# q and k stacked in device memory with one load per head, channel-mix pieces ended in their own step, and two banks each for up and down pieces in the tail

## The reference, cut to what matters

```
x2 = x + time_out                       # time mix
xc = ln(ln(x2)); xcs = shift(xc)
kc = square(relu(xcs @ Wck))            # 512 -> 2048, "up"
vc = kc @ Wcv                           # 2048 -> 512, "down"
A  = x2 + sigmoid(xc @ Wcr) * vc
q, k, v = rms(xn) @ Wq.T, Wk.T, Wv.T    # 16 heads of 32
attn = softmax(causal(q @ k.T / sqrt(32)))
x  = xn + (attn @ v) @ Wo.T             # "proj"
B  = x + sum over 2 of 8 experts of p_e * Wd_e(silu(Wg_e r) * (Wu_e r)),  r = rms(x)
```

## Time and profile before

| | |
|---|---|
| median of 3 runs | 2160.09 us (2159.92 to 2160.28) |
| the profiled execution's own time | 2173.18 us |
| its span | 2171.3 us |
| PE busy | 1872.4 us (86%) |
| PE weight loads busy | 1594.3 us (73%) |
| DVE, ACT, POOL busy | 1172.8, 1055.6, 524.8 us |
| mean granted clock of TensorE | 0.95 |
| phases, by the trace | time mix to about 270 us, projections to 435.7, heads to 1344.6, experts to the end |

### The profile page before, as it was taken

The page is one execution under the profiler, slowest core; times in us unless marked ns, Lnnn a source line. Parts: engine busy times, 40 slices in busy tenths (PEclk is TensorE's granted clock), DMA queues, the critical chain, the costliest instruction groups (busy, mean ns, idle before and its releaser), DMA issues. The chain is left out here.

```text
span 2171.3 us, 30573 instructions
## 1 busy us (share of the span) xinstructions
PE 1872.4 (86%) x10866; PEld 1594.3 (73%) x10866; DVE 1172.8 (54%) x1866; ACT 1055.6 (49%) x1758; POOL 524.8 (24%) x560
## 2 busy tenths in 40 slices
PE   3878679938989888989988754999999999999997
PEld 2666468726767766777766533999999999999986
DVE  6887332135667556666565423555555555555553
ACT  4454344223656555565655312555555555555553
POOL 3243200000000100100100151334344443534343
PEclk9989879969999999999999987999999999999999
DMA  4332345486354433743443314666666665756562
GB/s 174 117 116 97 137 173 193 153 275 142 101 144 114 113 105 112 159 123 100 107 112 101 90 25 148 221 203 204 197 208 209 206 214 196 229 202 205 192 193 49
DMA packets 124211, 334.38 MB, mean 154 GB/s; under 512 B 33743, under 2 KB 33743, under 8 KB 109858
## 3 DMA queue, kind: packets, MB, share of 16 engines
q1 hardware_dynamic: 101266, 291.69, 39.1%
q0 software_dynamic: 18272, 33.13, 9.3%
q10 hardware_dynamic: 4592, 8.52, 1.1%
HBM read 270.67 MB, written 75.06 MB: 159 GB/s over the span
## 5 line engine op out<-in xcount | busy, mean ns | idle before, releaser
L48 PE MATMUL bank<-ex_x_hi,ex_w_hi 128*128 128x256 f32 x1472 | 418.9, 285 | 5.2 <-issue 5.2
L50 PE MATMUL bank<-ex_x_hi,ex_w_lo 128*128 128x256 f32 x1472 | 417.2, 283 | 0.0
L49 PE MATMUL bank<-ex_x_lo,ex_w_hi 128*128 128x256 f32 x1472 | 417.2, 283 | 0.0
L1865 DVE TENSOR_TENSOR ex_w_lo<-ex_stage,ex_w_hi 128x2048 fp32r<-128x2048 f32 x138 | 249.9, 1838 | 147.6 <-ACT ex_w_hi L1810 144.6
L48 PEld LDWEIGHTS bank<-ex_x_hi,ex_w_hi 128*128 128x128 f32 x1472 | 282.9, 192 | 8.2 <-issue 5.6
L49 PEld LDWEIGHTS bank<-ex_x_lo,ex_w_hi 128*128 128x128 f32 x1472 | 283.1, 192 | 2.7
L50 PEld LDWEIGHTS bank<-ex_x_hi,ex_w_lo 128*128 128x128 f32 x1472 | 282.9, 192 | 0.0
L1750 POOL TENSOR_TENSOR ex_a_lo<-ex_a,ex_a_hi 128x256 fp32r<-128x256 f32 x184 | 177.6, 986 | 391.6 <-ACT ex_a_hi L1830 391.1
L1825 ACT ACTIVATE ex_gate<-bank 128x256 f32<-128x256 f32 x184 | 70.7, 384 | 240.0 <-PE bank L50 240.0
L1214 ACT ACTIVATE hd_p_full<-bank 128x512 f32<-128x512 f32 (+1 forms) x192 | 94.4, 528 | 140.7 <-PE bank L1506 139.9
L48 PE MATMUL bank<-hd_down_hi,hd_a_hi 128*128 128x512 f32 x256 | 112.1, 438 | 47.7 <-issue 22.8
(11 more groups left out here) (265 smaller groups left out, 4434.4 us busy)
## 6 DMA issues: line engine op xcount, KB each, us to landing
ex_stage<-in_w_moe SPq DMA_DIRECT2D x69, 1536.0 KB, 6.8
first_w<-in_w_moe SPq DMA_DIRECT2D x23, 1536.0 KB, 7.3
hd_raw<-in_w_up SPq DMA_DIRECT2D x64, 256.0 KB, 2.9
hd_raw<-in_w_dn SPq DMA_DIRECT2D x64, 256.0 KB, 2.8
hd_q<-scratch_q_hi SPq DMA_DIRECT2D x128, 64.0 KB, 2.6
hd_k<-scratch_k_hi SPq DMA_DIRECT2D x128, 64.0 KB, 2.5
tm_x_in<-in_x SPq DMA_DIRECT2D x4, 1024.0 KB, 7.5
scratch_xn<-tm_xn SPq DMA_DIRECT2D x4, 1024.0 KB, 5.2
```

Of the source, the lines that this page charges most:

```text
L48: pe.matmul(out, lhsT=w_hi, rhs=x_hi, start=first, stop=False)
L49: pe.matmul(out, lhsT=w_hi, rhs=x_lo, start=False, stop=False)
L50: return pe.matmul(out, lhsT=w_lo, rhs=x_hi, start=False, stop=last)
L1865: return dve.tensor_tensor(dst, src, hi.bitcast(F32), ALU.subtract)
```

## The change

Scratch tensors q_hi, q_lo, k_hi, k_lo become one, qk, laid out by sequence, part of a bank's rows, stacked row (96), column of heads, q or k, and token. project_phase stores into it with 24 transfers of 256 KB from 32 partitions per sequence where there were 4 of 1 MB: q_hi and k_hi are written twice. load_slot reads a head with one transfer of 384 KB (96 partitions, 4 KB each). SP's list at the start of heads_phase is put in another order, and the waits for constants move to their first use. ACT and DVE finish each piece right after its begin, in its own step, and ACT takes the relu before the weights. The tail's ups alternate between banks 5 and 4, its sums between banks 6 and 0, and PE waits for the piece before last there. The first down (and proj) of four waits for weights and blocks one by one.

```diff
+    TAIL = proj_at[B - 1]
     def turn_bank(b, j):
-        return psum[7] if b < B - 1 else psum[j]
+        return psum[7] if b < B - 1 else psum[1 + j % 3]
-        q2 = sb("q2", [P, SLOTS, S], F32R)
-        k2 = sb("k2", [P, SLOTS, S], F32R)
+        qk = sb("qk", [P, SLOTS, 2, S], F32R)
+        q2, k2 = qk[:, :, 0, :], qk[:, :, 1, :]
+        def up_bank(k):
+            return psum[4] if k >= TAIL and ups_before[k] % 2 else psum[5]
+        def sum_bank(k):
+            return psum[0] if k >= TAIL and sums_before[k] % 2 else psum[6]
# sync, heads_phase
             def load_slot(g):
-                (six transfers of 64 KB)
+                b, c, part = feature_rows(g)
+                sp.dma_start(qk[0:STACK, g % SLOTS, :, :].bitcast(F32), d["qk"][b, part, :, c]).then_inc(slot_in[g % SLOTS], 16)
+            load_slice(0)
             load_slot(0)
-            for w in range(RAW):
-                load_slice(w)
+            load_slice(1)
+            load_mix(0)
+            load_slice(2)
+            load_slice(3)
             load_slot(1)
-            load_mix(0)
-            for g in range(2, SLOTS):
-                load_slot(g)
+            load_slice(4)
+            load_slice(5)
+            for w in range(DEEP):
+                sp.wait_ge(w_lo_ready, w + 1)
+                load_slice(w + RAW)
+                load_slot(w + 2)
             (vecs, wr)
+            for g in range(DEEP + 2, SLOTS):
+                load_slot(g)
             (v, xn, gate)
-            for w in range(DEEP):
-                sp.wait_ge(w_lo_ready, w + 1)
-                load_slice(w + RAW)
# scalar: begin(k) takes the relu before the weights; the loop over steps
-                for k in late:
-                    finish(k)
                 for k in ks[:1]:
                     begin(k)
+                    finish(k)
                 (exps(i, 0), exps(i, 1))
-                for k in ks[:1]:
-                    finish(k)
                 ...
                 for k in ks[1:]:
                     begin(k)
+                    finish(k)
                 (max_row)
-                late = ks[1:]
# vector: the same; finish(k) of the first piece now ahead of maxima(s, 2) and low_v
# tensor
-                n = ups_before[k]
+                n = ups_before[k] - (k > TAIL + TT)
+                if k >= TAIL and n == ups_before[TAIL]:
+                    pe.wait_ge(o_ready, N // 2)
                 if n:
                     pe.wait_ge(a_full, n)
-            def total(k, left_hi, left_lo, j):
-                n = sums_before[k]
+            def total(k, left_hi, left_lo, j, ready):
+                n = sums_before[k] - (k > TAIL)
                 ...
                 for q in range(DEEP):
+                    if j == 0:
+                        ready(q)
             def down(k, b, c, j):
-                pe.wait_ge(w_lo_ready, slice_at["down", b, c, DEEP - 1] + 1)
-                pe.wait_ge(a_lo_ready, ups_before[k])
+                def ready(q):
+                    pe.wait_ge(w_lo_ready, slice_at["down", b, c, q] + 1)
+                    pe.wait_ge(a_lo_ready, ups_before[k] - DEEP + q + 1)
-            pe.wait_ge(consts_ready, CONSTS)
-            pe.wait_ge(const_in, 32)
# sync, project_phase
-            def features_out(name, src, b, out):
-                sp.dma_start(d[name][b].rearrange("c p s -> p c s"), src[:, :, :].bitcast(F32)).then_inc(out, 16)
+            def features_out(src, which, groups, b, out):
+                for part in range(HC):
+                    for g in groups:
+                        sp.dma_start(d["qk"][b, part, g * HD:(g + 1) * HD, :, which, :],
+                                     src[part * HD:(part + 1) * HD, :, :].bitcast(F32)).then_inc(out, 16)
```

More of the change, by code:

```diff
@@ L772, in feature_rows @@
         half, c, place = n // 8, n % 8 // 2, n % 2
-        return b, c, (half * 2 + place) * HD
+        return b, c, half * 2 + place
     def pair_cols(p):
@@ L997, in load_slot @@
             def load_slot(g):
-                b, c, row = feature_rows(g)
-                src = slice(row, row + HD)
-                for n, (qs, ks) in enumerate((("q_hi", "k_hi"), ("q_hi", "k_lo"), ("q_lo", "k_hi"))):
-                    at = slice(n * HD, (n + 1) * HD)
-                    sp.dma_start(q2[at, g % SLOTS, :].bitcast(F32), d[qs][b, c, src, :]).then_inc(slot_in[g % SLOTS], 16)
-                    sp.dma_start(k2[at, g % SLOTS, :].bitcast(F32), d[ks][b, c, src, :]).then_inc(slot_in[g % SLOTS], 16)
+                b, c, part = feature_rows(g)
+                sp.dma_start(qk[0:STACK, g % SLOTS, :, :].bitcast(F32), d["qk"][b, part, :, c]).then_inc(slot_in[g % SLOTS], 16)
             def load_v(p):
@@ L1068, in _ @@
                     load_xn(b)
-            for k in range(pieces_before(STEPS), PIECES):
+            for k in range(TAIL, PIECES):
                 follow(k)
@@ L1161, in begin @@
             def begin(k):
-                for w in fresh[k]:
-                    weight(w)
                 kind, b, c, m = order[k]
@@ L1167, in begin @@
                     act.wait_ge(up_done, n + 1)
-                    act.activation(relu[:, m, :], up_bank[:, :], ACT.Relu).then_inc(relu_ready, 1)
+                    act.activation(relu[:, m, :], up_bank(k)[:, :], ACT.Relu).then_inc(relu_ready, 1)
+                for w in fresh[k]:
+                    weight(w)
                 if k in turn_at:
@@ L1258, in _ @@
                 weight(w)
-            act.wait_ge(consts_ready, CONSTS)
-            act.wait_ge(const_in, 32)
-            late = []
             for s in range(STEPS):
@@ L1442, in _ @@
                 weight(w)
-            dve.wait_ge(consts_ready, CONSTS)
-            late = []
             for s in range(STEPS):
@@ L2049, in _ @@
                 sp.wait_ge(q_hi_ready, b * HC + HC)
-                features_out("q_hi", q_hi, b, q_hi_out)
+                features_out(q_hi, 0, (0, 1), b, q_hi_out)
                 sp.wait_ge(q_lo_ready, b * HC + HC)
-                features_out("q_lo", q_lo, b, q_lo_out)
+                features_out(q_lo, 0, (2,), b, q_lo_out)
                 sp.wait_ge(k_hi_ready, b * HC + HC)
-                features_out("k_hi", k_hi, b, k_hi_out)
+                features_out(k_hi, 1, (0, 2), b, k_hi_out)
                 sp.wait_ge(k_lo_ready, b * HC + HC)
-                features_out("k_lo", k_lo, b, k_lo_out)
+                features_out(k_lo, 1, (1,), b, k_lo_out)
                 sp.wait_ge(v_ready, b * TT + TT)
                 sp.dma_start(d["v"][b], v[:, :, :]).then_inc(v_out, 16)
-            for out in (q_hi_out, q_lo_out, k_hi_out, k_lo_out, v_out):
-                sp.wait_ge(out, 16 * B)
+            for out, copies in ((q_hi_out, 8), (q_lo_out, 4), (k_hi_out, 8), (k_lo_out, 4), (v_out, 1)):
+                sp.wait_ge(out, 16 * copies * B)
         @block.gpsimd
@@ L2096, in high @@
                     if b and m == 0:
-                        act.wait_ge(out, b * 16)
+                        act.wait_ge(out, b * 16 * 8)
                     act.activation(dst[:, m, :], psum[bank + m][:, :], ACT.Copy).then_inc(ready, 1)
@@ L2147, in low @@
                     if b and m == 0:
-                        dve.wait_ge(out, b * 16)
+                        dve.wait_ge(out, b * 16 * 4)
                     dve.tensor_tensor(dst[:, m, :], psum[bank + m][:, :], hi[:, m, :].bitcast(F32),
```

45 lines of the change are left out of this document (28 added, 17 removed).

## The result

| | before | changed |
|---|---|---|
| median, same chip (4 runs each) | 2160.01 us (2158.37 to 2160.28) | 2103.49 us (2099.81 to 2107.55) |
| the profiled execution's own time, its span | 2173.18, 2171.3 us | 2101.72, 2099.6 us |
| PE, DVE, ACT, POOL busy | 1872.4, 1172.8, 1055.6, 524.8 us | 1864.0, 1176.2, 1055.2, 520.0 us |
| mean granted clock | 0.95 | 0.956 |

What follows compares the result with a forecast made beforehand. Heads phase limits: late constants at the start, PE in the steps, a PE-ACT-DVE-PE bank chain in the tail, then POOL. From the median, 2160.1 - 20 + 2 - 32 - 2 - 26.5 = 2081.6, said as 2082 us; range 2058 to 2114.

Steps and rivals of the forecast that it cites:

- the wait for exps' third part: Heads steps, ACT: a wait for the third part of the turned scores would appear, under 0.5 us.
- The start: Start of heads phase: first up at about 446 instead of 466.25 us, released by the mix input; 20 us gained.
- The stores: Last projections sequence: more, narrower q and k stores delay v's store and the phase end by 0 to 6, taken as 2 us.
- Pieces end in their own step: Heads steps: earlier a_lo and block waits 28, clock 12, relu 4, less ACT's new wait 12; 32 us gained (5 to 44).
- the 12 of the clock: Heads steps, 520 to 1150 us: 12 of 19 us lost to lower granted clock go with PE's waits.
- The new wait of ACT: Heads steps: ACT waits after relu for DVE's a before exps(i, 0); 12 us lost over 59 steps (0 to 35).
- The tail: End of heads phase: second banks and earlier scatter make it 111 us against 151.7; 26.5 us gained without the 14.1.
- The 14.1 us: Tail: PE's 15.65 us wait less its usual 1.50, taken as belonging to the profiled execution alone and left out.
- the rival of the long wait: Tail: the long wait is in ordinary runs too and goes with the second bank; 2068 us, chance 0.12.
- ACT eating the middle: Heads steps: ACT's new wait costs 0.5 us or more per step, middle gains only about 10 us; 2104 us, chance 0.16.
- The stores' rival: Projections: port limits make stores cost 5 us in the last sequence and each of three others; 2100 us, chance 0.08.
- lock: Heads steps: ACT, DVE and PE wait in one ring, 1.5 us more per step, 88 us lost; 2170 us, chance 0.04.

Runs made afterwards that it cites:

- start alone: Kernel before with only SP's new start order and the constants' waits moved to first use, on chip A: 2174.26 us, ratio 0.9962.
- coarse waits: Changed kernel, but a chunk's first down waits at its start for the whole chunk, not block by block, on chip C: 2148.98 us, ratio 0.9836.
- the late one: Changed kernel with a step's second piece finished at the next step's start: 2119.00 us (A); with whole-chunk waits too, 2161.71 us (C).

## Why the prediction was right or wrong

The time fell inside the range, 21.5 us above the forecast: 56.5 us were gained where 78 were forecast. The direction and the four places of the gain were right. That the time stayed inside owes something to luck and to the range's width, for all three signs that the prediction named for being wrong came: PE's idle time in the steps is 58.2 us (43.2 of the 610 from 510 to 1120), not under 40; the scatter starts 50.8 us into the tail, later than 48; and v's store lands 8.0 us late, more than 6. Kept were the signs of the releaser, the downs (no wait for a_lo over 0.8 us), the clock (0.99) and the scatter without a gap; the wait for exps' third part reached 0.9 us, not under 0.5.

- **The start.** 18.7 us to the first up, forecast 20. Right as a step, and the releaser is the mix input as forecast; x_lo took 9.7 us to land, just outside the 7.3 to 9.3 of the earlier trace rows. (It is issued fifteen issues earlier in SP's list, not seven; the time of 2 us behind the phase's first issue was right.) What the sum left out: 6.8 us of an earlier start alone are given back within the stage (start alone). "So nothing is late" was wrong: slices are, ACT waits 16 to 18 us for one. That the copies of x make them late is not shown by the total: with the copies moved that stall goes, and the stage is 0.7 us shorter.
- **The stores.** Forecast 2 us in a range of 0 to 6, measured 8.1 between the first two traces, of which 7.1 behind the projections' first product, and 6.1 over all: the memset at 446.9 as the mean of nine profiles with narrow stores, at 440.7 as that of five with wide ones or those of before. I took the rate and the issue time of 128 partitions for 32. An issue took 1.2 us, not 0.4 to 0.46, so SP issued q's and k's stores of the last sequence without a gap from 409.99 to 436.3, v's store left 4.9 us late, and it took 6.9 us to land instead of 3.9. By the stretch 420 to 430 narrow stores move 232 GB/s at 0.94, which I estimate as 247 at full; wide ones 315 at 0.85, 371 at full. The Trainium skill (SBUF — State Buffer, "Door 1: The DMA port swizzle") says that a transfer reaches only the ports its partitions sit on, half of them for 32; the trace has two thirds. (Stores from different groups of 32 are in flight together there, which is a possible reason and not shown.) The rule pointed the right way, and its estimate of 5 was nearer than my 2.
- **Pieces end in their own step.** Forecast 32, and 2 for the tail's first piece. Measured are 29.3 us from the first up to the first proj: 20.4 of idle time, where 28 + 4 + 2 - 12 = 22 were forecast, and 9.0 of faster matmuls for the 12 of the clock. Against the start alone (on A) the other edits brought 36 us in the stage (733.5 less 697.3), so the size was right; its reason was not. The step that failed: "Now a_lo follows its a at once, some 2 us earlier than PE asks for it". With coarse waits it still made PE wait 13.3 us, and taken back alone it costs nothing. What took the 3.3 us waits away was the half sentence behind it, PE waiting block by block: 22 us beside the early finish, 40 beside the late one (737.0 on C less 696.9 on A). By that experiment the clock's share is 13.4 us, near the 12. The new wait of ACT was priced at 12; what goes when the finish is late again is 3.4 for p_full and 4.1 for the row of maxima. The other 6 us by which the wait for that row grew over the trace of before (3.1 to 13.0) have no cause shown.
- **The tail.** Forecast 111, measured 119.6 from the first proj's first matmul (1152.93). The scatter began 50.8 us after it, not 42: the eleven pieces took 40.4 us and not 32.4. Turned rows and logits take 5.4 of them, where the sum had 1.6; waits inside the first proj and the first down (0.62 and 1.56 us) and a stretch at half the clock near 1180 (0.72 over 1177 to 1183) are most of the rest. From the first scatter on, 68.9 us as forecast, and PE's stand was 5.45 for "about 5". The second banks are worth 17 to 20 us by experiment on a chip with the stall; 4.7 of them lie ahead of the scatter, and what they are worth without the stall is not shown.
- **The 14.1 us.** Leaving them out was right for this pair, but "the profiled execution alone" was a wrong reason: such waits are in every profile of chips A and C, where the kernel before took over 20 us more in ordinary runs too. The change's ratio is the same there (0.9746), and the second banks do not take the stall away. So the rival of the long wait fell for this pair, and on those chips its price isn't saved either.
- **The sum.** 21 us short between the two traces: stores 6.1, start 1.3, stage 4.7 (6.8 given back by the early start, less 2 that the other edits brought beyond their forecast), tail 8.6.
- **The rivals.** ACT eating the middle would have given 2104, the measured time, but for a reason that is not there: the middle's gain is nearly whole. That its number was hit is chance. The stores' rival had the right mechanism at one place, the last sequence, and not in the three before: PE's part of the projections lasts 141.7 us with narrow stores and without. No lock was seen.

## What to carry to other kernels

A wait for a whole chunk ahead of its first consumer is best split by block before anything is reordered: three quarters of the piece hide the producer's chain. An earlier start can be given back behind it, by transfers that do not follow and by a lower clock, so it is measured where the stage ends, not where it begins. A store cut into pieces should keep all 128 partitions: here 24 such stores let the heads begin as early as six.

## What the runs showed of the hardware that was not expected

- A store of 256 KB takes SP about 1.2 us to issue from 32 partitions and 0.46 from 128, with the queues at 0.94 and 0.85.
- On chips A and C DVE, ACT and PE stall under POOL's scatter of 32 indirect transfers in every profile; the changed kernel's tail is 17 us longer there (136.5 against 119.6). The kernel before took 2182 and 2180 us on them, against 2160 and 2161 in the first pair and on B. The stall is not the chip's alone: the first pair's profile of before has it, the changed kernel's has not, and it is that profile which took 13 us more than the ordinary runs. Within an up piece PE has no wait in its list, and yet stalled there for 1.7 us at a time; so it is not the program's semaphores alone. POOL itself is not slowed: from the first to the last of the 32 issues it takes 39.5 to 39.8 us in the eight profiles of A and C, and 41.5 to 42.0 in the five without a stall. What the stall is stays open, no run took the scatter away.
